# Half of the elementwise work of an RWKV and mixture-of-experts kernel given to GpSimd

## The reference

```python
# x: 8 x 4096 x 1024, float32
x_sh = pad(x by one step in time)
key, value = x*tmk + x_sh*(1-tmk), x*tmv + x_sh*(1-tmv)
r = sigmoid(x*tmr + x_sh*(1-tmr))
k, v, r = key @ Wk.T, value @ Wv.T, r @ Wr.T
# scan over time: q = max(u+k, w); e1 = exp(-w-q); e2 = exp(u+k-q)
#                 a = e1*a + e2*v;  b = e1*b + e2;  wkv = a/b
x = layernorm(x + (wkv * r) @ Wo.T + bo)
# mixture of experts: E = 8, F = 4096, top 2 of 8 by softmax
tgt2 = sum_e router_w[e] * (relu(x @ W1[e].T + b1[e]) @ W2[e].T + b2[e])
out = layernorm(x + layernorm(x + tgt2) * gamma + beta)
```

## Time and profile before

| | us |
|---|---|
| median of 2 runs | 10,549.72 |
| lowest and highest | 10,498.71 and 10,600.73 |
| the profiled execution's own time | 10,505.84 |
| its span on the slowest core (core 7) | 10,504.2 |
| spans of the 8 cores | 10,476.0 to 10,504.2 |
| busy in that span: PE, DVE, ACT, POOL | 8,329.2, 2,259.0, 1,788.4, 541.8 |

### The profile page before, as it was taken

One profiled execution on the slowest core, in us unless ns is written; L12 is line 12 of the kernel. 1 busy time (PEld: TensorE's weight loads), 2 busy tenths in 40 slices (PEclk: granted clock), 3 DMA queues, 4 the chain that ended last, 5 costly groups with the idle time before them and its releaser, 6 DMA issues.

```text
span 10504.2 us, 93818 instructions; the slowest of 8 cores (10476.0 to 10504.2 us)
## 1 busy us (share of the span) xinstructions
PE 8329.2 (79%) x37824; PEld 3810.3 (36%) x37824; DVE 2259.0 (22%) x3326; ACT 1788.4 (17%) x2368; POOL 541.8 (5%) x1032
## 2 busy tenths in 40 slices
PE   3666666559995799849996699939997599948997
PEld 2222222234442344324443344424443344423443
DVE  5000000241105211250114301161013410161102
ACT  1111001121121211112111121111211112112121
POOL 0000000000000000000000000000000000000000
PEclk7877887779997899969997899969998799979998
DMA  2655565413441244304441244303442144303442
GB/s 47 157 153 154 154 153 152 107 49 144 148 152 40 102 150 147 115 29 154 147 148 68 81 148 148 136 18 141 147 150 86 60 148 148 144 32 118 151 145 108
DMA packets 192744, 1256.30 MB, mean 120 GB/s; under 512 B 19513, under 2 KB 36154, under 8 KB 44354
## 3 DMA queue, kind: packets, MB, share of 16 engines
q0 software_dynamic: 148032, 1082.20, 31.9%
q1 hardware_dynamic: 44290, 168.11, 4.1%
HBM read 1241.84 MB, written 150.99 MB: 133 GB/s over the span
## 4 chain that ended last, share of the span: by engine, by line
PE 63%; DMA 19%; DVE 12%; issue 3%; ACT 3%; another core or an unknown queue 1%; DVEq 0%; POOLq 0%; SPq 0%; ACTq 0%; POOL 0%
PE psB L693 8%; PE psA L671 7%; PE psC L693 7%; PE psD L693 7%; PE psB L671 7%; PE psC L671 7%; PE psD L671 7%; PE psA L693 6%; DMA arena<-w2H 5%; DMA arena<-w1H 5%; DMA w2C<-arena 3%; DMA w1C<-arena 2%; DMA arena<-w1C 2%; DMA arena<-w2C 1%; PE psA L461 1%
## 5 line engine op out<-in xcount | busy, mean ns | idle before, releaser
L671 PE MATMUL psA<-x1bf,arena 128*128 128x512 bf16 x4096 | 1064.5, 407 | 318.9 <-DMA arena<-w1H 297.6
L702 DVE SCALAR_TENSOR_TENSOR otmp<-psC,b2s,rwbc 128x512 f32<-128x512 f32 x128 | 96.1, 751 | 4868.8 <-PE psC L693 4868.8
L676 ACT ACTIVATE arena<-psA,b1s 128x512 bf16<-128x512 f32 x512 | 351.8, 687 | 4622.9 <-PE psA L671 4622.9
L693 PE MATMUL psC<-arena 128*128 128x512 bf16 x4096 | 923.3, 385 | 113.1 <-ACT arena L676 54.9
L693 PE MATMUL psD<-arena 128*128 128x512 bf16 x4096 | 935.1, 388 | 93.3 <-DMA arena<-w2H 92.5
L671 PE MATMUL psB<-x1bf,arena 128*128 128x512 bf16 x4096 | 1006.3, 390 | 0.0
L693 PE MATMUL psB<-arena 128*128 128x512 bf16 x4096 | 937.8, 389 | 80.9 <-DMA arena<-w2H 71.9
L693 PE MATMUL psA<-arena 128*128 128x512 bf16 x4096 | 938.6, 389 | 74.4 <-DMA arena<-w2H 73.4
L671 PE MATMUL psC<-x1bf,arena 128*128 128x512 bf16 x4096 | 967.8, 379 | 0.0
L671 PE MATMUL psD<-x1bf,arena 128*128 128x512 bf16 x4096 | 967.8, 379 | 0.0
L671 PEld LDWEIGHTS psA<-x1bf,arena 128*128 128x128 bf16 x4096 | 404.8, 102 | 926.6 <-issue 531.3
(11 more groups left out here) (147 smaller groups left out, 4973.4 us busy)
## 6 DMA issues: line engine op xcount, KB each, us to landing
arena<-w1C POOLq DMA_DIRECT2D x448, 1024.0 KB, 5.1
arena<-w2C POOLq DMA_DIRECT2D x448, 1024.0 KB, 5.1
arena<-w1H POOLq DMA_DIRECT2D x64, 1024.0 KB, 8.4
w1C<-arena SPq DMA_DIRECT2D x64, 1024.0 KB, 4.4
arena<-w2H POOLq DMA_DIRECT2D x64, 1024.0 KB, 8.4
w2C<-arena SPq DMA_DIRECT2D x64, 1024.0 KB, 4.4
xch<-xH SPq DMA_DIRECT2D x16, 1024.0 KB, 8.4
outH<-tgt SPq DMA_DIRECT2D x8, 2048.0 KB, 8.1
```

Source lines behind the costliest of these rows:

```text
L671: grp = p.op("tensor", lambda e, jd=jd, fc=fc, buf=buf, bk=bk: e.matmul(bank[bk][:, 0:TQ], w1s[buf][:, jd, fc * 128:(fc + 1) * 128], x1bf. ...
L676: t_hev = p.op("scalar", lambda e, jf=jf, e_=e_, bk=bk: e.activation(hsb[:, jf, :], bank[bk][:, 0:TQ], AF.Relu, bias=b1s.ap()[:, e_:e_ + 1 ...
L693: grp = p.op("tensor", lambda e, jf=jf, buf=buf, bk=bk: e.matmul(bank[bk][:, 0:TQ], w2s[buf][:, jf, :], hsb[:, jf, :], start=(jf == 0), st ...
L702: t_ot = p.op("vector", lambda e, bk=bk, e_=e_, dc=dc: e.scalar_tensor_tensor(otmp[:], bank[bk][:, 0:TQ], b2s.ap()[:, e_:e_ + 1, dc:dc + 1 ...
```

## The change

The change gives POOL a share of DVE's elementwise work, in four forms.

- A helper `half_op` records one operation twice: feature groups 0 to 3 on DVE, groups 4 to 7 on POOL, both with the same waits. It is used for the difference (L304), `sW` (L397), d1 (L412), e1 (L416), y (L420), wkv (L446), the cast (L480), the two `x1` ops and the `x1bf` cast (L529, L532, L535), and in the tail for the cast (L726), the two broadcast ops (L776, L779) and the second `tgt2 += x1` (L791). Gamma and beta (L785) go 4 to DVE and 4 to POOL. Whoever used the result now waits for both halves. The scans stay on DVE; those after y wait only for y's own half.
- The 24 mixing ops of a chunk: 12 stay on DVE, fused; each of the other 12 becomes a multiply and an add on POOL, the add waiting for the multiply.
- In the W2 loop the write into `tgt2` goes from DVE to POOL, where it stands behind the load of the next slab and ahead of the one after.
- For expert 0 this write is `otmp + x1`, and the first `tgt2 += x1` (L720) is gone.

The rest of the diff hands lists of tokens on where there was one. The core of it:

```diff
+        def half_op(fnmk, waits, engs=("vector", "gpsimd")):
+            tv = p.op(engs[0], fnmk(0, 4), waits=waits, inc=engs[0])
+            tp = p.op(engs[1], fnmk(4, 8), waits=waits, inc=engs[1])
+            return (tv, tp)
...
-                    t_mk = p.op("vector", lambda e, j=j: e.scalar_tensor_tensor(
-                        j2(kbf, j), j2(sA, j), vcol(V_TMK, j), j2(xch, j, 0, C),
-                        ALU.mult, ALU.add), waits=[t_xd], inc="vector")
+                    h_ = j // 4
+                    if h_ == 0:
+                        t_mk[0] = p.op("vector", lambda e, j=j: e.scalar_tensor_tensor(
+                            j2(kbf, j), j2(sA, j), vcol(V_TMK, j), j2(xch, j, 0, C),
+                            ALU.mult, ALU.add), waits=[t_xd[0]], inc="vector")
+                    else:
+                        tk = p.op("gpsimd", lambda e, j=j: e.tensor_scalar(
+                            j2(kbf, j), j2(sA, j), vcol(V_TMK, j), None, ALU.mult),
+                            waits=[t_xd[1]], inc="gpsimd")
+                        t_mk[1] = p.op("gpsimd", lambda e, j=j: e.tensor_tensor(
+                            j2(kbf, j), j2(kbf, j), j2(xch, j, 0, C), ALU.add),
+                            waits=[tk], inc="gpsimd")
...
                 t_rsig = p.op("scalar", lambda e: e.activation(rbf, sB, AF.Sigmoid),
-                              waits=[t_mr], inc="scalar")
+                              waits=[t_mr[0], t_mr[1]], inc="scalar")
...
-                t_W = p.op("vector", lambda e: e.tensor_add(sW, sB, sC),
-                           waits=[t_Ls, t_m], inc="vector")
+                t_W = half_op(lambda lo, hi: (lambda e: e.tensor_add(
+                    sW[:, lo:hi, :], sB[:, lo:hi, :], sC[:, lo:hi, :])),
+                    [t_Ls[0], t_Ls[1], t_m])
...
-                        waits=[t_y, t_d2, t_Lc], inc="vector")
+                        waits=[t_y[h_], t_d2, t_Lc], inc="vector")
...
                     if e_ == 0:
-                        t_tg = p.op("vector", lambda e, tg=tg: e.tensor_copy(tg, otmp[:]),
-                                    waits=[t_ot, last_tgt2_use], inc="vector")
+                        t_tg = p.op("gpsimd", lambda e, tg=tg, dc=dc: e.tensor_add(
+                            tg, otmp[:], x1.ap()[:, dc, :]),
+                            waits=[t_ot, last_tgt2_use] + t_x1_ready, inc="gpsimd")
                     else:
-                        t_tg = p.op("vector", lambda e, tg=tg: e.tensor_add(tg, tg, otmp[:]),
-                                    waits=[t_ot], inc="vector")
+                        t_tg = p.op("gpsimd", lambda e, tg=tg: e.tensor_add(tg, tg, otmp[:]),
+                                    waits=[t_ot], inc="gpsimd")
...
-            t_z2 = p.op("vector", lambda e: e.tensor_add(tgt2.ap(), x1.ap(), tgt2.ap()),
-                        waits=[t_tgt2_done, t_x1_ready], inc="vector")
+            t_z2 = t_tgt2_done
```

More of the change, by code:

```diff
@@ L244, in tapout @@
                 tt = tap_t[name]
+                w = list(wait) if isinstance(wait, list) else [wait]
                 tok = p.dma("sync", lambda e, ap=ap, tt=tt: e.dma_start(tt.ap(), ap),
-                            waits=[wait], inc="out")
+                            waits=w, inc="out")
                 p.tap_gate = tok
@@ new lines, in build @@
+                for j in range(JD):
+                    h_ = j // 4
+                    if h_ == 0:
+                        t_mv[0] = p.op("vector", lambda e, j=j: e.scalar_tensor_tensor(
+                            j2(vbf, j), j2(sA, j), vcol(V_TMV, j), j2(xch, j, 0, C),
+                            ALU.mult, ALU.add), waits=[t_xd[0]], inc="vector")
+                    else:
+                        tk = p.op("gpsimd", lambda e, j=j: e.tensor_scalar(
+                            j2(vbf, j), j2(sA, j), vcol(V_TMV, j), None, ALU.mult),
+                            waits=[t_xd[1]], inc="gpsimd")
+                        t_mv[1] = p.op("gpsimd", lambda e, j=j: e.tensor_tensor(
+                            j2(vbf, j), j2(vbf, j), j2(xch, j, 0, C), ALU.add),
+                            waits=[tk], inc="gpsimd")
@@ new lines, in build @@
+                for j in range(JD):
+                    h_ = j // 4
+                    if h_ == 0:
+                        t_mr[0] = p.op("vector", lambda e, j=j: e.scalar_tensor_tensor(
+                            j2(sB, j), j2(sA, j), vcol(V_TMR, j), j2(xch, j, 0, C),
+                            ALU.mult, ALU.add), waits=[t_xd[0]], inc="vector")
+                    else:
+                        tk = p.op("gpsimd", lambda e, j=j: e.tensor_scalar(
+                            j2(sB, j), j2(sA, j), vcol(V_TMR, j), None, ALU.mult),
+                            waits=[t_xd[1]], inc="gpsimd")
+                        t_mr[1] = p.op("gpsimd", lambda e, j=j: e.tensor_tensor(
+                            j2(sB, j), j2(sB, j), j2(xch, j, 0, C), ALU.add),
+                            waits=[tk], inc="gpsimd")
@@ L474, in build @@
                             vcol(V_BO, jd), j2(xch, jd, 1, C + 1), ALU.add, ALU.add),
[L475 removed]
+                            waits=[grp[1], t_wkv[0], t_wkv[1]], inc="vector")
                     blast[bk] = t_z0v
@@ L786, in ln_pass @@
                             j2(src_ap, j), j2(src_ap, j), vcol(V_GAM, j), vcol(V_BET, j),
-                            ALU.mult, ALU.add), waits=[t_a2], inc="vector")
+                            ALU.mult, ALU.add), waits=[t_a2[h_]], inc=eng)
                 return t_last
-            t_ln1 = ln_pass(tgt2.ap(), t_z2, apply_gb=True)
-            t_z3 = p.op("vector", lambda e: e.tensor_add(tgt2.ap(), x1.ap(), tgt2.ap()),
-                        waits=[t_ln1], inc="vector")
-            last_x1_use = t_z3
@@ L794, in build @@
-            t_ln2 = ln_pass(tgt2.ap(), t_z3, apply_gb=False)
+            t_ln1 = ln_pass(tgt2.ap(), [t_z2], apply_gb=True)
+            t_z3 = half_op(lambda lo, hi: (lambda e: e.tensor_add(
+                tgt2.ap()[:, lo:hi, :], x1.ap()[:, lo:hi, :], tgt2.ap()[:, lo:hi, :])),
+                list(t_ln1))
+            last_x1_use = list(t_z3)
+            t_ln2 = ln_pass(tgt2.ap(), list(t_z3), apply_gb=False)
             t_out = p.dma("sync", lambda e, q=q: e.dma_start(
                 outH.ap()[:, :, q * TQ:(q + 1) * TQ], tgt2.ap()),
-                waits=[t_ln2], inc="out")
+                waits=list(t_ln2), inc="out")
```

183 lines of the change are left out of this document (97 added, 86 removed).

## The result

| | before | changed |
|---|---|---|
| median of all executions | 11,132.84 us (10) | 11,474.77 us (11) |
| executions compared | 10,494.8 to 10,600.7 (4) | 11,019.7 to 11,034.2 (5) |
| ratio of these | | 1.0477, 95% interval 1.0424 to 1.0531 |
| profiled execution, own time | 10,505.84 | 11,039.42 |
| its slowest core's span | 10,504.2 (core 7) | 11,037.9 (core 0) |

The changed kernel is 4.8% slower: 534 us on the profiled executions, where the prediction had 491. The plain median of 11,475 lies above the stated range of 10,600 to 11,200; the five executions compared lie inside it.

A forecast was written before the change was run, and what follows sets the result against it. PE was taken to bound the cached expert stage, a serial chain with no full engine the stretches between. Attention 307, tail 92 and cached experts 92 summed to +491 on 10,505.8, giving 10,997 us; range 10,600 to 11,200.

The forecast's parts named there:

- the cached experts: Expert stage from the weight cache: POOL's add delays the w2C loads and PE waits, +92 us over 56 experts.
- Slack 1.2: PE stands 0.55 us: Cached W2 loop: a load 1.76 us later, against 1.2 us of slack, stops PE for 0.55 us.
- every second group stops: 3 per expert: Cached W2 loop: a stop gives the next load room, so groups 2, 4, 6 stop; 168 x 0.55 = +92 us.
- The tail: End of each block: the fold's saving against dearer casts, broadcast ops, gamma and beta; +11.5 us, times 8: +92 us.
- Turns: Paired halves on DVE and POOL: no overlap, a pair costs both halves, 1.3 us more; 10,997 us, chance 0.58.
- POOL's price, twice DVE's time: POOL's elementwise ops: two sources 1.22 us for 512 elements, 2.29 for 1024, 4.43 for 2048; one source half of that rate.
- Mixing: Attention's mixing: POOL's chain of multiplies and adds, in turns with DVE, takes 21.7 us against 12.0, +9.7 a chunk.
- A chunk: One attention chunk: mixing, full-width pairs and casts together +19.2 us, times 16: +307 us.
- Block 0's expert stage: Block 0's experts: loads wait for each cache write, so an add of 1.2 us on POOL fits; 0 us.
- side by side: Rival for the paired halves: DVE and POOL overlap, sum +148 us, 10,654 us; chance 0.22.
- the fast POOL: Rival: POOL as fast as DVE and overlapping with it, sum -233 us, 10,270 us; chance 0.05.
- Slow POOL: Rival: POOL three times slower than DVE, halves in turns, sum +993 us, 11,499 us; chance 0.15.

The follow-up runs named there:

- x4: The changed kernel with DVE's half of each pair made to wait for POOL's half; 11,087.8, 11,096.9 and 11,189.4 us, 1.0589 of before.
- x3: The changed kernel with the weight-cache loads of blocks 1 to 7 issued by SP instead of POOL, the add left on POOL; 10,814.6 and 10,860.3 us.
- x1: The changed kernel with the writes into tgt2 back on DVE, expert 0's still as otmp + x1; 10,836.1 us in one execution.
- x2: The kernel before with only the writes into tgt2 moved to POOL, expert 0's as a copy; 10,666.5 to 10,692.6 us, ratio to before 1.0165.
- x8: The kernel before with the fold, the sigmoid's mixing first and the next block's xch load ahead of the output store; 10,296.4 and 10,298.5 us, ratio 0.9801.

## Where the prediction was right and where it failed

Direction and mechanisms came out as forecast: the halves take turns, POOL works at half DVE's rate, and the add delays the loads behind it. Three terms of the sum were mis-sized, and that +491 lies near +534 is partly luck: attention came out 20 us lower and the tail 54 lower, the cached experts 108 higher and block 0 9 higher. The step that failed most is the one on the cached experts, "Slack 1.2: PE stands 0.55 us" and "every second group stops: 3 per expert", in all +92 us. It measured +200: 0.8 us for a stop and 3.7 late loads per expert. The tail, +92, measured +38. The stated range failed for a reason of its own: it was laid around one profiled execution of 10,505.8 us and has no term for the spread of executions. Ten executions of the kernel before went from 10,494.8 to 11,583.5 us with a median of 11,132.8, and the eleven of the changed one from 11,019.7 to 11,920.3, with the median above the range's upper end. By its own steps:

- **Turns** (the likeliest case). Shown by the asymmetric rows above and by x4. The Trainium skill, SBUF — State Buffer, section "SBUF: two separate sides", has it as an exclusive lock between a VectorE op with two SBUF inputs and a GpSimd op that reads SBUF. The rows agree to 0.2 us: 3,390 ns on whichever engine came second, where the halves alone, 1,225 and 2,350 (x4), add to 3,575. A pair was forecast at +1.3 us; `sW` measured +1.1 (3.39 for 2.29).
- **POOL's price, twice DVE's time.** 1.22 forecast for the 512-element add, 1.26 measured; 2.29 for 1,024, 2.34 to 2.36 measured alone in five ops and 1.89 to 2.17 in three; 4.43 for 2,048, 4.49 measured. The 0.1 us for "a crossing between engines" was misread: both rows, 5003.59 and the one that ends at 5003.48, are DVE's. From DVE's otmp to POOL's add it is 0.15 (5247.24 after 5247.09).
- **Mixing**: forecast +9.7 us, measured +12.6 (24.6 for 12.0). Two terms were off and partly cancelled. The multiply was sized at 0.43 and takes 0.92: 12 x 0.49 = 5.9 more. The turns were charged to POOL (6.0 less 2.4), but DVE bore them: its fused ops took 829, 671 and 702 ns on average where each of the 24 took 478 or 479 before, and DVE was not on the path; POOL's multiplies took 1,150 and 943 beside it and 922 alone.
- **A chunk**: +19.2 forecast, +18.0 measured (19.2 by the medians of the cores). With 12.6 in the mixing, 5.4 are left to pairs and casts, forecast at 9.5. d1's POOL half was only 1.89 us, e1's pair mostly stayed beside ACT, and the cast (L524) on POOL takes 1.04 us alone, not 1.22. A cost that the sum did not have is the scan behind y: in the chunk above its eight instructions take 7.14 us (at 4756.64) where they took 5.25, so that from y's start to the end of that scan it is 0.8 us more, in place of 1.3 for y's pair.
- **The tail**: +11.5 forecast, +4.0 to 4.8 measured. The terms that failed are those of the two casts (+2.6), the four broadcast ops (+9.6) and gamma and beta (+0.9). POOL's cast of 2,048 takes 1.89 us alone and 2.93 beside DVE's, so a cast costs +0.6 to 0.7, not 1.3. In the first broadcast op POOL starts while DVE is still copying the second factor out of PSUM, so the pair begins 1.3 us before the single op could have (4546.49 and 4547.85 in the fence of x3) and costs some 1 us, not 2.4. And DVE's gamma and beta ops lie beside POOL's half of the second broadcast op (from 4555.71 on in that fence): the two steps together took 10.53 us in the changed kernel for 8.38 before, +2.15 in place of 3.3.
- **The cached experts**: +92 us forecast, +200 measured, the largest miss. That the load leaves 1.76 us later was right (1.74). "Slack 1.2: PE stands 0.55 us" was not: a stop delays PE by 0.8 us (7.71 and 7.69 for 6.91), so only 0.94 of the slack could be used. The slack was counted from the landing to the group's start, but a group doesn't start on the landing itself: the load issued at 5248.45 landed at 5253.58, after 5.13 us and not 5.0, and its group began at 5253.71. "Every second group stops: 3 per expert" was too few: after a stop the next load has next to no slack either (5260.63 follows 0.13 us after its landing), and landings scatter from 5.0 to 10.4, so 203 late loads in 54 experts are 3.7 per expert. From the first W2 group's start to the last one's an expert takes 51.9 us on average, where it took 48.7: 3.2 of the 3.57. Another 0.2 come from w1C loads (27.1 us of waits for 16.7), and 0.15 weren't assigned. The queue is the cause by x1, x2 and x3.
- **Block 0's expert stage**: 0 forecast, 9 measured; what they are was not looked into.
- **The fold**: -4.5 a block forecast, 35 us for eight measured by itself.

Of the rivals, side by side falls with x4, and the fast POOL with its rows. Slow POOL (three times DVE's rate) did not hold for two-source ops.

## What to carry to other kernels

Before elementwise work is split between DVE and GpSimd, ask whether both halves read SBUF: here their times nearly added, 1.22 and 2.35 us to 3.39, for an op that DVE alone did in 2.29. Ask next what is queued behind the instruction that is moved: here a 1.3 us add, off every path by itself, delayed each prefetch by 1.7 us where 0.9 could be spared. A serial stretch may be shortened by order (what feeds the next engine first, a load ahead of a store) or by folding one op into another: x8 took 2.0% off with the two, no arithmetic on GpSimd, where the split added 4.8%.

## What the runs showed of the hardware

- POOL's multiply with a per-partition coefficient took 922 ns for 256 elements, and its multiply and add with two coefficients 914 ns for 512 (L837 in x3), while a two-source op of 256 took 650 to 680. The Trainium skill's GPSIMD Engine Reference, section "Engine selection", has one-input ops roughly at line rate; the casts agree (1,037 ns for 1,024 elements, 1,891 for 2,048, that is 0.83 ns for each further element, where DVE's two-source ops need 1.04), these multiplies don't. What their fixed part is was not tried.
- POOL's two-source 128x1024 ops weren't alike: 1,893 ns for the difference and for d1, which read one buffer twice, shifted by one element, 2,339 to 2,357 for five ops on two buffers, and 2,172 for e1 (L455), which also reads two (x4). Why is open.
- Beside a POOL op DVE's copies out of PSUM kept their 0.69 us, and its two-source SBUF op stretched from 2.29 to 5.29: the second fence of x3, 4547.24 and 4547.85, both inside POOL's 4546.49 to 4550.99 at their start. One-source SBUF ops give way too: 6.65 us for four gamma and beta ops of 512 elements in that tail, 1.66 each (4555.71), where eight had taken 3.75, and DVE's scans went from 730 to 960 ns (L470).
- Loads from the cache landed in 4.9 us (median) when SP issued them and 5.1 when POOL did, and a cached expert took 113.4 us with the one and 114.3 with the other, in kernels with no arithmetic on POOL.
